# Where the first cross product of a chunked recurrence stands among the other work of TensorE

## The reference

```python
def step(St, inp):
    kt, qt, vt, at, bt = inp
    Sk = jnp.einsum('bhij,bhj->bhi', St, kt)
    err = Sk - vt
    Sn = at[..., None] * St - (bt[..., None] * err)[..., None] * kt[:, :, None, :]
    ot = jnp.einsum('bhij,bhj->bhi', Sn, qt)
    return (Sn, ot)
```

## Time and profile before

| | us |
|---|---|
| median of 3 runs (2569.99 to 2586.25) | 2571.39 |
| the profiled execution | 2565.11 |
| its span, first to last instruction | 2563.5 |
| TensorE busy | 2015.8 (79%) |
| VectorE busy | 1777.7 (69%) |
| ScalarE busy | 1172.9 (46%) |
| mean granted TensorE clock | 0.869 |

### The profile page before, as it was taken

The page is one execution under the profiler, slowest core; times in us unless marked ns, Lnnn a source line. Parts: engine busy times, 40 slices in busy tenths (PEclk is TensorE's granted clock), DMA queues, the critical chain, the costliest instruction groups (busy, mean ns, idle before and its releaser), DMA issues. The chain is left out here.

```text
span 2563.5 us, 40439 instructions
## 1 busy us (share of the span) xinstructions
PE 2015.8 (79%) x12402; PEld 1377.4 (54%) x12402; DVE 1777.7 (69%) x4427; ACT 1172.9 (46%) x2737; POOL 944.3 (37%) x969
## 2 busy tenths in 40 slices
PE   7999999999467777766665664466999958898994
PEld 4444444444355555555454553355788833566773
DVE  4888888888577887878877676656656517774444
ACT  1665656665356665555554443454333200313442
POOL 0444444444423322222222122211444436345774
PEclk7999999999687888777777776778999979899896
DMA  2666666666457789999999999975322251207985
GB/s 85 125 121 128 127 119 126 127 126 120 108 135 189 209 228 238 240 231 262 283 274 278 265 298 256 303 203 161 100 70 70 86 207 31 74 8 249 283 233 147
DMA packets 641632, 443.55 MB, mean 173 GB/s; under 512 B 294997, under 2 KB 594981, under 8 KB 636197
## 3 DMA queue, kind: packets, MB, share of 16 engines
q1 hardware_dynamic: 526536, 271.03, 41.4%
q0 software_dynamic: 40672, 128.75, 19.4%
q10 hardware_dynamic: 74240, 41.58, 5.6%
HBM read 238.76 MB, written 194.04 MB: 169 GB/s over the span
## 5 line engine op out<-in xcount | busy, mean ns | idle before, releaser
L995 ACT ACTIVATE p_diag_o<-p_ident,p_gd 128x128 f32<-128x128 f32 x1152 | 360.9, 389 | 313.5 <-PE p_ps_o L948 290.5
L398 DVE SCALAR_TENSOR_TENSOR p_y<-p_ps_proj,p_w,p_y 128x508 f32<-128x508 f32 (+2 forms) x576 | 416.1, 741 | 117.6 <-ACT p_y L310 104.1
L948 PE MATMUL p_ps_o<-p_ws,p_diag_o 128*128 128x128 f32 x1792 | 331.1, 349 | 142.5 <-ACT p_diag_o L995 64.9
L948 PEld LDWEIGHTS p_ps_o<-p_ws,p_diag_o 128*128 128x128 f32 x1792 | 295.1, 250 | 201.0 <-ACT p_diag_o L995 71.9
L243 PE MATMUL p_ps_proj<-p_x,p_w 128*128 128x512 f32 x768 | 342.8, 596 | 2.7 <-ACT p_beta_t L301 2.7
L907 PE MATMUL p_ps_z<-p_turned,p_gcol 112*32 112x128 f32 x3584 | 149.9, 309 | 219.4 <-DMA p_turned<-history 219.2
L206 POOL TENSOR_TENSOR p_kq<-p_y,p_sig 128x512 f32<-128x512 f32 x128 | 162.3, 1271 | 360.6 <-ACT p_sig L321 359.8
L907 PEld LDWEIGHTS p_ps_z<-p_turned,p_gcol 112*32 112x32 f32 x3584 | 101.8, 122 | 276.0 <-DMA p_turned<-history 238.1
L630 DVE SCALAR_TENSOR_TENSOR p_zo<-p_ws,p_gd,p_zo 128x128 f32<-128x128 f32 x768 | 240.0, 347 | 3.4
L243 PEld LDWEIGHTS p_ps_proj<-p_x,p_w 128*128 128x128 f32 x768 | 142.0, 192 | 158.0 <-issue 154.9
L774 POOL DMA_DIRECT2D p_near_t<-gram x128 | 67.0, 548 | 320.4 <-PE p_ps_x L932 317.3
(11 more groups left out here) (263 smaller groups left out, 3843.1 us busy)
## 6 DMA issues: line engine op xcount, KB each, us to landing
p_w<-in_wguT SPq DMA_DIRECT2D x64, 480.0 KB
history_sums<-p_sums ACTq DMA_DIRECT2D x112, 256.0 KB, 5.9
p_zo<-history_sums POOLq DMA_DIRECT2D x28, 1024.0 KB, 11.6
history<-p_hist SPq DMA_DIRECT2D x9, 2048.0 KB, 12.2
history<-p_late SPq DMA_DIRECT2D x9, 2048.0 KB, 14.2
decays<-p_dec SPq DMA_DIRECT2D x64, 256.0 KB, 2.3
beta_v<-p_bv SPq DMA_DIRECT2D x64, 256.0 KB, 2.5
gram<-p_gram SPq DMA_DIRECT2D x64, 256.0 KB, 3.7
```

The source lines that it names most:

```text
L398: nc.vector.scalar_tensor_tensor(out=yv[:, :, s:], in0=pv[:, :, 0:T - s], scalar=par[j % 2][:, kind, TAPS - 1 - s:TAPS - s], in1=yv[:, :, ...
L948: nc.tensor.matmul(ps_o[s // 4 % 2][:, s % 4, :], diag_o[p // DO % NDO][:, p % DO, :], rows[:, r, :], start=(s % 4 == 0 and r == 0), stop= ...
L995: last = nc.scalar.activation(diag_o[n % NDO][:, p % DO, :], ident[:], ACT.Copy, scale=gd[g][:, r, s:s + 1])
```

## The change

In TensorE's loop the first cross product, `near_product(at, 0)`, moves ahead of `own_rows(at, 7)`, and the three units that stood behind row 7 move behind `near_product(at, 1)`, where six then stand in a row. ScalarE's list follows: the copies `near_rows(at, 0)` stand ahead of the diagonals and the bank copy that belong to row 7, and one of its stores of unit results comes after the second copies. No instruction is added or taken away.

```diff
-    UNITS_AFTER = (0, 0, 1, 2, 2, 2, 3, 3)
+    UNITS_AFTER = (0, 0, 1, 2, 2, 2, 3)
...
-                for s in range(HALF):
+                for s in range(HALF - 1):
                     own_rows(at, s)
                     while u < min(units, sum(UNITS_AFTER[:s + 1])):
                         history(at - 1, u)
                         u += 1
                 pe.wait_ge(near_g_made, at + 1)
                 near_product(at, 0)
+                own_rows(at, HALF - 1)
                 near_turn(at, 0)
                 near_product(at, 1)
...
-                for s in range(HALF):
+                for s in range(HALF - 1):
                     made = past(s, made)
...
                 near_rows(at, 0)
+                made = past(HALF - 1, made)
                 near_rows(at, 1)
```

## The result

| | before | after |
|---|---|---|
| median of the runs timed together, us | 2578.6 | 2638.74 |
| ratio, 95% interval | | 1.0263 [1.0225, 1.0301] |
| profiled execution, us | 2565.11 | 2640.61 |
| its span, us | 2563.5 | 2639.0 |
| mean granted TensorE clock | 0.869 | 0.860 |

The change makes the kernel slower by 2.6% (+68 us by that ratio): 60 us between these medians, 75 us between the two profiled executions. The forecast had +39 us: the sign was right, the amount half of what the traces show. The time stands at the upper end of the range.

The account below looks back on a forecast made before the run. The bound was taken as a chain of waits, no engine being full. Order and loads +30, ScalarE +4 and spill +5 us gave +39 us on 2571.4 us, so 2610 us, range 2572 to 2642 us.

Parts of the forecast that it names:

- order and loads, with L: TensorE, unit 10 to row 8 in 14 leaves: total shift 14 L - 31.5 us, +30 us at L = 4.4 us.
- L: Time from the issue of unit 15's rows on SP to their landing: taken as 4.4 us, bounds 2.6 and 6.5 us.
- unit 15's rows issued after unit 10's start: SP's issue of the last unit's row loads: 2.00 us after unit 10's start, as in leaf 3 before.
- unit 15: TensorE's last history unit, run after its load lands and ahead of the second turn: 0.5 us.
- second turn: TensorE's turn of the second cross product, between unit 15 and row 8: 1.0 us.
- step 3: VectorE in a leaf's second half, released by row 8: its wait for TensorE rises from 0.3 to 4 or 5 us.
- ScalarE's copy: First cross product's copies, behind the copy of units 8 and 9: +2.3 us in leaf 11, about 1 in two more, +4.
- a leaf's start, the spill: Spill on SP leaves 4.76 us later; leaves 11, 13 and 14 shift 4.8 us instead of 3.0, +5 us.
- I take no wait: First product's operand near_w on TensorE: its DMAs late by some tenths in late leaves at most, so no wait counted.
- B: Rival: last two units' loads land quickly, L 2.2 to 3.2 us, -1 to +13 us, no change; chance 0.26.
- C: Rival: loads are no limit, unit 10 to row 8 takes 8.67 us, -26 us, 2545 us; chance 0.08.
- D: Rival: history sums also late, VectorE waits 2 us more at 9 leaf starts, +57 us or more, 2630 us; chance 0.18.

Follow-up runs that it names:

- experiment 1: Kernel before with only the three units moved behind the second product, row 7 still ahead of the first product: ratio 1.0333 to the kernel before, +85 us.
- experiment 3: Loads of units 14 and 15 left out, unit 13's operands reused: changed kernel 0.9738 (2506.20 us), kernel before 0.9847 (2526.97 us), both against the kernel before.
- experiment 4: Kernel before, TensorE's order untouched, with one more wait on SP so units 14 and 15's loads are asked for after the second product: 1.0341, +88 us.
- experiment 5: Changed kernel, but units 14 and 15 load only 16 rows each: ratio 1.0188 to the kernel before, +48 us.
- experiment 6: Changed kernel, with TensorE repeating the products of units 13 and 14 for as long as it waited there for loads: ratio 1.0222 to the kernel before.
- experiment 8: Changed kernel with the second turn and row 8 ahead of units 14 and 15: ratio 1.0043 to the kernel before, +11 us.
- experiment 9: Changed kernel with three other splits of the units around the turns and row 8, leaves 0 and 15 as before: 1.0065, 1.0012 and 1.0027 to the kernel before.

## Why the prediction was right in sign and half in size

The mechanism was the forecast's, and experiments 1, 3 and 4 show it: the last two loads are asked for when unit 10 is through, nothing long stands between any more, and row 8 comes late behind them. Laid leaf by leaf beside the timeline of before, the recurrence is 82.2 us longer; the stages behind it are 6.7 us shorter, for which the change offers no reason. The terms, in us; those of the trace are sums over the leaves, measured against what the forecast took for each:

| term | forecast | in the trace |
|---|---|---|
| order and loads, with L | +30 (L 4.4) | +33 (L 4.6) |
| unit 15's rows issued after unit 10's start | 2.0 each | 2.4 each, +6 |
| unit 15 | 0.5 each | 0.94 each, +6 |
| second turn | 1.0 each | 1.76 each, +11 |
| row 8 to step 3 (0.42 to 0.67 us) | 0 | +3 |
| ScalarE's copy | +4 | +7 |
| first turn to unit 10, and row 7, the rest | 0 | +1 |
| a leaf's start, the spill | +5 | +9 |
| leaves 0 and 15 | 0 | +6 |
| sum | +39 | +82 |

**The views.** Right: VectorE is released twice, and the second release has nothing to spare. The turned product's wait fell by 33 us (some 30 said), and that was worth nothing, since step 3 waited longer by more.

**L.** Right, 4.6 us against 4.4, as a mean of the leaves; it was found by a middle of two bounds, so that it came this near is in part luck, and it hides a spread: it grows with the rows, 3.0 us in leaf 3 and 6.0 us in leaf 13. The Trainium skill, page "DMA: Bandwidth & Descriptors", section "Anatomy of one DMA", has a fixed 2.0 us and the bytes at 436 GB/s, measured for DMAs that GpSimd issues; these come from SP. By it the short loads of experiment 5 (64 KB of rows) would land in an estimated 2.15 us; 2.57 us were measured from issue to run, near it. For the 384 KB of leaf 11 it would be an estimated 2.9 us, and 5.5 us were measured, as were 4.17 us for the 64 KB of leaf 2: there the page is too short, and the measurement decides.

**The step that failed** stands in the prediction as "unit 15 (0.5 us) and the turn (1.0 us) follow". Both durations were rows of a TensorE that had not waited. After the waits that the prediction itself forecast (2 to 4 us a leaf; 2.1 to 5.9 came), unit 15 takes up to 1.02 us and the turn 1.76 us at a granted clock of 0.50. Together with the row behind them this is 20 us, the largest single part of what was missed, and experiment 6 takes nearly all of it away (the turns' part falls from 11 to 1 us). The Trainium skill, page "TensorE: Matmul & The Clock Gate", section "HAM oscillation — how this bites in real kernels", describes it: a DMA wait lets the clock fall, so that the work behind each wait starts cold. The trace agrees, with a granted 0.50 in the turn of leaf 13 behind waits of 4.05 and 0.94 us, and leaf 3 shows the same behind shorter ones (1.63 and 0.76 us). The rule spoke against this change; the prediction had the idle time and didn't follow it to the clock.

**Issue of unit 15's rows.** 2.00 us after unit 10's start was leaf 3's; the mean of the 14 leaves was 2.3 us before already. In seven leaves it is now 2.3 to 3.4 us; in three of them (5, 8, 11) an issue of SP just ahead of it takes 1.2 to 1.8 us in place of 0.4. Over all leaves that is another 6 us.

**ScalarE.** TensorE stands 0.7 to 2.2 us before the first turn in four leaves (5, 9, 12, 14), 6.6 us in all, where 4 us in three leaves were said. Leaf 11, from which the 2.3 us were worked out, has no such wait.

**The spill.** +5 us in leaves 11, 13 and 14 were said; the starts of these three changed by -0.1, 0.0 and -1.2 us. +10.6 us came, all in leaf 12. VectorE in that leaf, behind the rows that wait for the spill, first the issue of the spill and of the rows, then the wait:

```profile
1500.19 15.68 SPq L872 DMA_DIRECT2D history<-p_late  x3
...
1536.41 0.32 SPq L867 DMA_DIRECT2D p_turned<-history  x1
```

```profile
1558.29 0.96 DVE L624 TENSOR_TENSOR p_ws<-p_ws,p_dec 128x768 f32<-128x768 f32 x1 [16.10 <-PE p_ps_o L948]
```

Before, this wait was 4.21 us and the spill was issued at 1445.27, 11.9 us ahead of row 8 of leaf 11; now it goes 7.8 us ahead of it. The later issue is 4.1 us of the difference, and the rows behind the spill follow 36.2 us after it in place of 33.1; the rest is open, and no run tested this chain by itself. The place was a chain already known from the earlier trace rows, only one leaf on.

**The ends.** Leaves 0 and 15 have no units, and TensorE comes to the cross product early there: in the kernel before, row 7 started only 0.9 us behind POOL's first DMA into `near_w` in leaf 0 and 0.3 us ahead of it in leaf 15, and 10.3 us or more behind it in the 14 others. The operand isn't there yet. The first product of leaf 15 (its second half of 8 records) before, then the whole of it in the changed kernel:

```profile
1754.13 1.16 PE L921 MATMUL p_ps_n<-p_near_g,p_near_w 128*128 128x128 f32 x8 [0.89 <-DMA p_near_w<-p_w]
```

```profile
1831.40 4.08 PE L921 MATMUL p_ps_n<-p_near_g,p_near_w 128*128 128x128 f32 x16 [5.24 <-issue]
```

The profile names no releaser for these 5.24 us; in leaf 0 the same wait is 3.52 us and is put down to the DMA of `near_w`. So the product doesn't end sooner for standing first, and row 7, which used to fill this wait, now stands between it and its turn: 3.3 and 2.9 us. The prediction counted 14 leaves and left these out.

**near_w.** "I take no wait" was right for the 14 leaves with units, where no product waits to start, and wrong for the two ends. The first product itself took 2.95 us on average of the 14, not 1.88, since it is now the work that follows unit 9's wait (3.58 us in leaf 3, at a granted clock of 0.50); row 7 and its bank are shorter by as much (2.8 us in place of 4.0), so this cost nothing.

**The rivals.** B falls by the issue-to-run times. C falls as a forecast, but the medians of experiment 3 show its gain, 20.8 us, where the loads are gone. D's wait didn't come here, 19.5 us before and after, but it decides experiments 8 and 9. The change has two prices and takes one or the other: with the units ahead of row 8 they hold up step 3, behind it they hold up the sums.

## What to carry to other kernels

When work is taken from between a request and its use, compare the distance that is left, in microseconds, with the time that a load of that size takes under load, and read this in each stage, since the size grows. When a wait of some us is predicted on TensorE, price what runs behind it at half clock too (here 1.76 us in place of 1.01), up to the next place that releases another engine. And before a wait is shortened, look at the next wait of the same engine for how much slack it has: here there was none, since step 3 already waited 0.3 us, and the gain of 33 us ended there.

## What the runs showed of the hardware

- TensorE's clock falls after short waits too. In leaf 3 of the changed kernel two waits of 1.63 and 0.76 us, with 0.6 us of work between them, stood ahead of a turn of 1.76 us. In leaves 4, 7, 9 and 11 of experiment 5 waits of 1.5 to 2.2 us in sum left it at 0.99 us, and in leaf 3 of that run waits of 1.95 us in sum did not (1.77 us). So no limit is read off here.
- Products that compute nothing new hold the clock: experiment 6 ran 4 to 12 repeats a leaf, and in 13 of 14 leaves the turn behind them took what it takes without a wait (1.00 us). The wait itself stays.
- In experiment 5, loads of 64 KB of rows were used 2.1 to 2.8 us after their issue in leaves 3 to 13, though the DMA engines are busy for 0.83 of the recurrence there (690 to 1780 us of that run); in the changed kernel large ones took up to 6.0 us. The 960 KB by which two units' loads of leaf 13 exceed the short ones (2 x (448 + 112) KB against 2 x 80 KB) cost 3.4 us more (6.02 against 2.62 us from issue to run); by these two numbers an estimated 290 GB/s for all of them together.
